# Diffusion transformer blocks on one core: keys and self queries as products of 512 columns, and another order of the steps

## The reference

```
shift_sa, scale_sa, gate_sa, shift_ff, scale_ff, gate_ff = split(silu(cond) @ ada_w + ada_b, 6)
x = x + gate_sa * (attn(LN(x) * (1 + scale_sa) + shift_sa; qkv_w) @ sa_proj_w + b)
x = x + attn(q from LN(x), k and v from ctx, masked) @ ca_proj_w + b
x = x + gate_ff * (gelu((LN(x) * (1 + scale_ff) + shift_ff) @ fc1_w + b) @ fc2_w + b)
```

## Time and profile before

| | us |
|---|---|
| median of 3 runs | 1639.54 (1636.42 to 1641.39) |
| the profiled execution | 1635.45 |
| its span, first to last instruction | 1633.6 |
| mean granted clock of TensorE, as a share | 0.985 |
| busy: PE / DVE / ACT / POOL | 1470.9 / 1116.5 / 951.1 / 719.8 |
| PE share of the chain that ended last | 62% |
| "issue" share of it | 9% |

### The profile page before, as it was taken

One profiled execution on the slowest core, in us unless ns is written; L12 is line 12 of the kernel. 1 busy time (PEld: TensorE's weight loads), 2 busy tenths in 40 slices (PEclk: granted clock), 3 DMA queues, 4 the chain that ended last, 5 costly groups with the idle time before them and its releaser, 6 DMA issues.

```text
span 1633.6 us, 44574 instructions
## 1 busy us (share of the span) xinstructions
PE 1470.9 (90%) x17632; PEld 1282.0 (78%) x17632; DVE 1116.5 (68%) x2407; ACT 951.1 (58%) x1754; POOL 719.8 (44%) x982
## 2 busy tenths in 40 slices
PE   5979999999999999999888889989898898989987
PEld 4868878788887878888787777868778787887867
DVE  5557766666776666667766777677777767677654
ACT  3456565666656566665656646566565566656543
...
DMA packets 34251, 49.38 MB, mean 30 GB/s; under 512 B 3488, under 2 KB 24928, under 8 KB 34048
## 3 DMA queue, kind: packets, MB, share of 16 engines
...
...
## 4 chain that ended last, share of the span: by engine, by line
PE 62%; DVE 18%; ACT 9%; issue 9%; POOL 1%; SPq 0%; DMA 0%; DVEq 0%; ACTq 0%; POOLq 0%
PE score_t L676 8%; PE score L655 6%; PE p_unit L549 6%; PE p_unit L745 5%; PE p_mix L718 5%; PE p_unit L551 4%; PE p_unit L550 4%; DVE neg_max L1119 4%; PE p_out L549 3%; PE p_out L551 3%; PE p_out L550 3%; DVE hid_hi L1164 2%; PE p_mix L580 2%; DVE hid_lo L1166 2%; PE p_turn L735 2%
## 5 line engine op out<-in xcount | busy, mean ns | idle before, releaser
L1119 DVE TENSOR_REDUCE neg_max<-score 128x8 f32<-128x1024 f32 x224 | 273.8, 1222 | 115.2 <-PE score L655 109.7
L655 PE MATMUL score<-k_t,q_t 32*128 32x256 f32 x1792 | 254.5, 401 | 41.3 <-DVE q_less L1129 14.2
L676 PE MATMUL score_t<-q_less,k_t 32*128 32x128 f32 x3584 | 264.9, 287 | 11.5 <-ACT probs_t L977 6.1
L676 PEld LDWEIGHTS score_t<-q_less,k_t 32*128 32x128 f32 x3584 | 222.1, 189 | 23.3 <-issue 21.1
L979 ACT ACTIVATE probs_t<-score_t 128x1024 f32<-128x1024 f32 x168 | 172.0, 1024 | 94.4 <-PE score_t L676 81.7
L655 PEld LDWEIGHTS score<-k_t,q_t 32*128 32x128 f32 x1792 | 163.7, 188 | 77.7 <-issue 36.6
L1323 POOL TENSOR_TENSOR xt_lo<-xt,xt_hi 128x256 fp32r<-128x256 f32 x128 | 94.7, 740 | 261.8 <-ACT xt_hi L903 260.3
L898 ACT ACTIVATE xt<-p_mix,mod_now 128x128 f32<-128x128 f32 x384 | 154.3, 454 | 91.9 <-PE p_mix L580 60.6
L745 PE MATMUL p_unit<-w_out,heads_t 128*128 128x256 f32 x512 | 145.2, 407 | 21.0 <-ACT q_t L942 8.2
L549 PE MATMUL p_out<-w_hi,hid_lo 128*128 128x256 f32 x512 | 151.5, 296 | 0.8 <-issue 0.8
L1166 DVE TENSOR_TENSOR hid_lo<-hid,hid_hi 128x256 fp32r<-128x256 f32 x256 | 145.1, 567 | 8.8
...
## 6 DMA issues: line engine op xcount, KB each, us to landing
...
```

What stands on the lines that cost most here:

```text
L655: mm = pe.matmul(score_banks(b, h)[:, r % 2, t * 2 * N:(t + 1) * 2 * N].rearrange("p (e n) -> p e n", e=2), q_t[s][rows(r), t, tokens], k_ ...
L676: mm = pe.matmul(turned_banks(b, h)[:, r % 2, x * N:(x + 1) * N], k_t[s][rows(r), t, e, tokens], q_less[rows(r), j % 2, t, e, :], start=Tr ...
L1119: dve.tensor_reduce(by_half[:, 2 * h:2 * h + 2, 0:CT, :], score_banks(b, h)[:].rearrange("p r (t e n) -> p r t e n", t=CT, e=2), AX.X, ALU ...
```

## The change

Keys of both attentions and self queries become "by tile": such a unit holds one block of 128 features for all 4 batches, 2 x 3 = 6 products of 512 columns, where it held two blocks for 2 batches. They need the normed rows of all 4 batches, and the first round of an attention needs both key units (and both self query units). ACT and DVE move such a unit in one operation of 512 columns in place of two of 256; POOL's rotation takes the same number of elements in another shape.

The order changes on every engine. ACT moves a unit one step later, but first in that step (`ACT_UNIT` 1); then keys, context, gelus, exps, modulation, heads, mix, and the table loads last. On PE turn_heads moves ahead of norm, turn_max behind the MLP, the first norm ahead of turn_back. DVE scales keys first in a step, and heads ahead of z; POOL rotates ahead of the inverse roots and casts the context last. Units move (`UNIT_STEPS`), the MLP's 32 items stand in steps 36 to 43 and not 36 to 45, so a group ends two steps earlier; the keys' lag is 3; the context is split in step 20 and not 22; the copies of the modulation rows move; z of the first norm stands in the step of its transpose. In group 0 the statistics begin at step -16, the gates at -6, and the low weights of chunk 0 come at step -8, behind the first modulation.

```diff
-ACT_MIX, ACT_UNIT, ACT_MOD, ACT_HI = 0, 0, 0, 0
-DVE_KEYS, DVE_LOW, DVE_SCALE, DVE_SWAP, DVE_OUT = 1, 4, 1, 1, 0
+ACT_MIX, ACT_UNIT, ACT_MOD, ACT_HI = 0, 1, 0, 0
+DVE_KEYS, DVE_LOW, DVE_SCALE, DVE_SWAP, DVE_OUT = 1, 3, 1, 1, 0
...
-KEYS_LAG = 4
-FIRST_STATS, FIRST_Z, FIRST_LNT = -12, -11, -10
-AT_CTX = -4
+KEYS_LAG = 3
+FIRST_STATS, FIRST_Z, FIRST_LNT = -12, -10, -10
+EARLY_STATS = -16
+AT_CTX = -6
...
-MOD_AT = (-15, -1, 24)
+MOD_AT = (-20, -9, 26)
...
+def by_tile(unit):
+    return unit[0] == "k" or unit[:2] == ("q", SELF)
...
-UNIT_STEPS = ((-6, -5, -1, 2, 3, 4, 6, 7, 11, 14, 16, 18),
-              (-6, -5, -1, 2, 3, 4, 6, 7, 11, 14, 16, 17))
+UNIT_STEPS = ((-6, -5, -3, -1, 2, 4, 6, 7, 11, 15, 16, 18),
+              (-6, -5, -4, -2, -1, 4, 6, 7, 11, 14, 16, 17))
...
-MLP_COUNTS = ((2, 0, 3, 8, 2, 6, 7, 2, 1, 1), (2, 1, 2, 7, 6, 5, 5, 2, 1, 1))
+MLP_COUNTS = ((2, 1, 9, 3, 1, 4, 9, 3), (2, 3, 13, 0, 4, 1, 5, 4))
...
-GATES_AT, MOD_FF_AT, BIAS_AT, MOD_LN_AT, MOD_ROWS_AT = -1, 2, 6, 10, 11
+GATES_AT, MOD_FF_AT, BIAS_AT, MOD_LN_AT, MOD_ROWS_AT = -6, 4, 6, 10, 13
...
-FIRST_LO_DVE_AT = {-10: 0, -4: 1, 6: 3}
+FIRST_LO_DVE_AT = {-8: 0, -4: 1, 6: 3}
...
-PE_ORDER = ("round", "max", "proj", "norm", "mlp", "back", "turn", "first", "mix", "unit")
+PE_ORDER = ("round", "proj", "turn", "norm", "mlp", "max", "first", "back", "mix", "unit")
...
                 else:
-                    pe.wait_ge(xt_hi_made[s], group * 4 + 2 * half + 2)
-                    pe.wait_ge(xt_lo_made[s], group * 4 + 2 * half + 2)
+                    batches = GB if by_tile(UNITS[n]) else 2 * half + 2
+                    pe.wait_ge(xt_hi_made[s], group * 4 + batches)
+                    pe.wait_ge(xt_lo_made[s], group * 4 + batches)
...
-                for part in range(2):
+                for part in range(1 if by_tile(UNITS[n]) else 2):
                     for c in range(CT):
+                        if by_tile(UNITS[n]):
+                            mm = product(p_unit[:], w(col, c, stride, at + half * P, P), (hi[:, c, :], lo[:, c, :]),
+                                         c == 0, c == CT - 1)
+                            continue
...
             def scores(group, s, b, h):
 
                 if b % 2 == 0 and h == 0:
-                    half = b // 2
-                    pe.wait_ge(keys_low, group * 4 + 2 * s + half + 1)
-                    pe.wait_ge(keys_high, group * 4 + 2 * s + half + 1)
-                    pe.wait_ge(queries_made, group * 4 + 2 * s + half + 1)
+                    if b == 0:
+                        pe.wait_ge(keys_low, group * 4 + 2 * s + 2)
+                        pe.wait_ge(keys_high, group * 4 + 2 * s + 2)
+                    pe.wait_ge(queries_made, group * 4 + 2 * s + (2 if s == SELF else b // 2 + 1))
                     if b == 0 and s == CROSS and group:
...
                     for group, step in live(t):
-                        for s, b in batch_at(step, AT_TURN_MAX):
-                            turn_max(group, 4 * s + b)
-                    for group, step in live(t):
                         for s, b in batch_at(step, AT_PROJ):
                             project(group, s, b)
+                    for group, step in live(t):
+                        for s, b in batch_at(step, AT_TURN_Q):
+                            turn_heads(group, 4 * s + b)
...
                     for group, step in live(t):
+                        for s, b in batch_at(step, AT_TURN_MAX):
+                            turn_max(group, 4 * s + b)
+                    for group, step in live(t):
+                        for b in first_at(step, FIRST_LNT):
+                            turn_z(group, 0, b)
+                    for group, step in live(t):
                         for s, b in batch_at(step, AT_TURN_BACK):
                             turn_back(group, 4 * s + b)
-                    for group, step in live(t):
-                        for s, b in batch_at(step, AT_TURN_Q):
-                            turn_heads(group, 4 * s + b)
-                    for group, step in live(t):
-                        for b in first_at(step, FIRST_LNT):
-                            turn_z(group, 0, b)
                     for group, step in live(t):
...
-                    last = (group - 1) * 8 + 4 * s + 2 * half + 2
...
+                elif unit[:2] == ("q", SELF):
+                    act.activation(q_t[s][:, half, :], p_unit[:], ACT.Identity, scale=SCALE,
+                                   bias=bias_cols[:, 4 + half:5 + half]).then_inc(queries_made, 1)
...
                 else:
-                    for t in range(CT):
-                        op = act.activation(k_t[s][:, t, 0, cols], p_unit[:, t * HALF:(t + 1) * HALF], ACT.Identity,
-                                            scale=head_mask[:, 0:1], bias=key_bias[:, 0, 2 * s + t:2 * s + t + 1])
-                    op.then_inc(keys_low, 1)
+                    act.activation(k_t[s][:, half, 0, :], p_unit[:], ACT.Identity, scale=head_mask[:, 0:1],
+                                   bias=key_bias[:, 0, 2 * s + half:2 * s + half + 1]).then_inc(keys_low, 1)
...
                     for group, step in live(t):
+                        if step - ACT_UNIT in UNIT_AT[layer_of(group)]:
+                            move_unit(group, UNITS.index(UNIT_AT[layer_of(group)][step - ACT_UNIT]))
+                    for group, step in live(t):
+                        if layer_of(group) == 1 and step in KEYS_AT:
+                            low_keys(group, KEYS_AT[step])
+                    for group, step in live(t):
                         if step == AT_CTX:
                             split_ctx(group)
                         if (group, step) in SPLIT_AT:
                             new_weights((group, step))
                     for group, step in live(t):
-                        if layer_of(group) == 1 and step in KEYS_AT:
-                            low_keys(group, KEYS_AT[step])
+                        for n in GELU_AT[layer_of(group)].get(step, ()):
+                            gelu(group, n)
                     for group, step in live(t):
                         for s, b, h in turned_score_at(step):
                             exps(group, s, b, h)
                     for group, step in live(t):
-                        for n in GELU_AT[layer_of(group)].get(step, ()):
-                            gelu(group, n)
+                        for k, b in normed_at(step, AT_LNT + ACT_MOD, FIRST_LNT + ACT_MOD):
+                            modulate(group, k, b)
+                    for group, step in live(t):
+                        for s, b in batch_at(step, AT_TURN_BACK + ACT_HI):
+                            move_heads(group, 4 * s + b)
+                    for group, step in live(t):
+                        for s, b in batch_at(step, AT_MIX + ACT_MIX):
+                            move_mix(group, 4 * s + b)
...
                             act.activation(primed[:], cond[:, 0, 0:1], ACT.Exp)
-                    for group, step in live(t):
-                        for s, b in batch_at(step, AT_TURN_BACK + ACT_HI):
-                            move_heads(group, 4 * s + b)
-                    for group, step in live(t):
-                        for s, b in batch_at(step, AT_MIX + ACT_MIX):
-                            move_mix(group, 4 * s + b)
-                    for group, step in live(t):
-                        for k, b in normed_at(step, AT_LNT + ACT_MOD, FIRST_LNT + ACT_MOD):
-                            modulate(group, k, b)
-                    for group, step in live(t):
-                        if step - ACT_UNIT in UNIT_AT[layer_of(group)]:
...
                 dve.wait_ge(keys_low, group * 4 + 2 * s + half + 1)
-                for t in range(CT):
-                    op = dve.tensor_scalar(k_t[s][:, t, 1, half * HALF:(half + 1) * HALF],
-                                           p_unit[:, t * HALF:(t + 1) * HALF], head_mask[:, 1:2],
-                                           key_bias[:, 1, 2 * s + t:2 * s + t + 1], ALU.mult, ALU.add)
-                op.then_inc(keys_high, 1)
+                dve.tensor_scalar(k_t[s][:, half, 1, :], p_unit[:], head_mask[:, 1:2],
+                                  key_bias[:, 1, 2 * s + half:2 * s + half + 1], ALU.mult, ALU.add).then_inc(keys_high, 1)
 
...
                 for t in STEPS:
-                    if t in FIRST_LO_DVE_AT:
...
+                    for group, step in live(t):
+                        if layer_of(group) == 1 and step in KEYS_AT:
+                            high_keys(group, KEYS_AT[step])
+                    for group, step in live(t):
+                        for s, b in batch_at(step, AT_TURN_Q + DVE_SCALE):
+                            scale_heads(group, 4 * s + b)
                     for group, step in live(t):
                         for k, b in normed_at(step, AT_Z, FIRST_Z):
                             normalise(group, k, b)
                     for group, step in live(t):
```

(12 more changed lines are left out.)

42 lines of the change are left out of this document (19 added, 23 removed).

## The result

The kernel after takes 1628.12 us (median of 6 runs, 1624.81 to 1633.55), the kernel before 1638.45 in the same runs (1636.42 to 1641.39). The ratio is 0.9942 [0.9927, 0.9957]: 10 us faster, where 44 were forecast (1594 against 1638 to 1640). The profiled execution took 1624.81 us, span 1623.0, mean granted clock 0.962 (before: 0.985).

What follows compares the result with a forecast made beforehand. PE, busy 90% of the span, was taken as the bound. 8 x 2.8 (layer 0) + 8 x 3.1 (layer 1) = 47.2 us less, 2 more: profiled 1635.45 to 1590.2; median 4.1 above, 1594. Range 1566 to 1636.

Steps and rivals of the forecast that it cites:

- The products' 0.42: Six of twelve units, as 6 products of 512 columns for 12 of 256, save PE 0.42 us a group.
- 0.6 + 0.33 + 0.42 - 0.4: Layer 0: shorter evictions at steps 20-21 (0.6) and 6-7 (0.33), wide products (0.42), less the key unit's four-batch wait (0.4).
- The statement on steps 19 and 20: Layer 0: PE's waits of 0.30 and 0.25 us for the maximum and exps would go; 0.55 us gained.
- the moved MLP fillers of steps 18 and 19: Layer 1: MLP products taken from these steps return only part of their 1.4 us; 1.0 us a period lost.
- The gains of the list: Layer 1: six PE gaps (1.35, 0.85, 0.76, 0.73, 0.64, 1.16 us) would go, 5.49 us a period.
- The splits of step 12: Layer 1: DVE's hidden-unit splits, held by POOL's rotation of cross keys, come late; 0.9 us booked, bounds 0 and 3.
- The 0.25 and 0.3 booked around step 21: Layer 1 losses: the round behind the first key unit waits for DVE (0.25 us); step 21's shuffle delays a maximum (0.3).
- Start: Earlier modulation and statistics gain up to 2.6 us, but first scores need four units, all batches; loss of 2 taken.
- Rival 1: POOL's work from step 18 to round 1 binds layer 1 and eats its gain: 1619 us; chance 0.13.
- Rival 2: Layer 1: POOL's rotations each wait for the previous one's key scaling, slipping over 6 us: 1646 us; chance 0.12.
- Rival 3: Waits only move: filler from steps 18 and 19 costs 1.4 us in both layers, key unit waits 1.5: 1637; chance 0.06.
- Rival 4: Wide products run at the far faster pitch, 0.55 us a unit more, times 96: 1541 us; chance 0.04.

Runs made afterwards that it cites:

- last experiment: The second kernel with layer 0's second key unit in step 22 and not 23: 1607.93 us, ratio 0.9828 to the kernel before.
- fourth: The kernel after with every unit by halves again (256 columns), the new order kept: 1623.4 us, ratio 0.9914 to the kernel before.
- fifth experiment: The second kernel with layer 0's last two MLP items also moved to steps 18 and 19: 1609.34 us, ratio 0.9831 to the kernel before.
- first kernel: The kernel after with useless PE transposes added in layer 1, 12 in step 18 and 6 in step 19: 1618.71 us, ratio 0.9889.
- the second: The kernel after with two of layer 1's four step-17 MLP items put back to steps 18 and 19: 1604.96 us, ratio 0.9802.
- the sixth: The kernel before with only the change's new MLP counts, so the MLP ends at step 17: 1647.13 us, ratio 1.0066.
- third kernel: The kernel after with POOL's two sums of the MLP output in layer 1 one step later: 1619.52 us, ratio 0.9903 to the kernel before.
- eighth experiment: The kernel of the fifth experiment with DVE's layer 1 shuffle behind the maximum's subtraction: 1636.14 us, ratio 1.0006 to the kernel before.
- ninth kernel: The second kernel with the gate products of group 0 at step -1 again, not -6: 1603.38 us, ratio 0.98 to the kernel before.

## Why the prediction was wrong

The direction and the range held (1628 lies in 1566 to 1636), the size did not: 10 us for 44. By its steps:

- **Layer 0: right in its sum, in part by luck.** 2.8 us a period were forecast, 2.4 came (95.34 to 92.95). The products' 0.42 are 0. Other terms missed and cancelled. Shown: the wait at step 24 is filled by the unit of step 23 (0.7 us, last experiment), the eviction and the width, less the wait for four batches, give 0.3 (fourth), where 0.6 + 0.33 + 0.42 - 0.4 was booked. ACT and DVE take 0.776 and 0.803 us for a key unit, 0.61 less than the two pairs of the earlier trace rows, where 0.7 was taken (groups by line and shape, kernel after):

```profile
L963 ACT ACTIVATE k_t<-p_unit,key_bias,head_mask 128x512 f32<-128x512 f32 x32 | 24.8, 776 | 23.9 <-PE p_unit L560 23.9
```

```profile
L1102 DVE TENSOR_SCALAR k_t<-p_unit,head_mask,key_bias 128x512 f32<-128x512 f32 x32 | 25.7, 803 | 26.9 <-ACT k_t L963 26.9
```

The statement on steps 19 and 20 was wrong: instead of going, 0.30 and 0.25 became 1.05 and 0.26. It cost little, as the fifth experiment shows, for a round there follows the maximum in any case. The other way went the norm of step 13, whose 0.29 us for z closed without being booked, the projection, 0.56 for 0.42, and the 0.25 for steps 4 and 6, of which no row is left.
- **Layer 0, what is missing.** 6 x -2.8 = -16.8 was forecast, -9.2 came: 2.1 are the products in five periods, 3.2 the sixth, at the seam, which got 0.4 longer where 2.8 less was forecast, and 2.2 the two periods at a clock of 0.98.
- **Layer 1: the step that failed.** It is the sentence "the moved MLP fillers of steps 18 and 19 return only part of their 1.4 us (1.0 lost)". The gains of the list did come: the six gaps closed, and PE's idle time fell by 2.37 us a period where the terms for waits gave 5.49 - 2.8 = 2.69. But PE's busy time, forecast 0.42 lower, rose by 2.25. The working priced the filler as PE time that overlaps a wait. It had no term for what an idle PE does to its own clock, 1.25 us a period, and none for POOL's queue, 1.34. Together the moved items cost 2.6 us a period, not 1.0; with them back the period is 95.6, 2.7 under that of before. The clock's share is shown by the first kernel, whose periods differ from the kernel after behind the key unit alone. That moving the items costs time, in the old order too, is shown by the second (23 us less) and the sixth (11 us more).
- **POOL's queue.** The output sums follow the MLP, and now stood ahead of a rotation and of the low part that ACT waits for. That queue was not walked through at step 19. That it holds the key unit's input is shown by the third kernel, where the input ends 1.26 us earlier.
- **Layer 1, smaller terms.** The unit of step 20 waits 0.38 us for the booked 0.35, but only because PE comes late to it; at the full clock it waits 1.44 (first kernel). The splits of step 12 take 1.37 to 1.52 us each under POOL's rotation, in place of 0.28 and 0.43, as forecast, and PE waits 0.63 us for one where 0.9 was booked. The round of step 3 now waits 0.78 us for the queries less their maximum; before, it had no such row, and units stood in steps 2 and 3. The prediction booked the like of it in layer 0 only. The 0.25 and 0.3 booked around step 21 have no rows.
- **Start: -3 to +5 with a loss of 2 taken, +1.0 measured** at the first Exp load. This can't be called right or wrong. Six runs have the code of the kernel after up to there (it, the first, second, third, fifth and eighth), and their first Exp load stands at 184.86 to 192.58 us, the kernel before's at 186.91. Their first round is 5 to 8 us later than before; much of it is made up.
- **The end: 0 forecast; the last stretch is 1.8 us longer**, with as many products (592) and a clock of 0.83 for 0.88. The second and the ninth kernel, with the same code there, take 68.00 us at 0.90 and 65.84 at 0.95. So this row too is the clock's, and differs from run to run.
- **Rival 1 (POOL binds layer 1)** is not what happened: POOL's last addition ends 0.9 us ahead of round 1, by its walk 0.8. But its mechanism is real and near, as the eighth experiment shows: there its price is 3.3 us a period, and it begins at step 20, ahead of where the rival looked. **Rival 2**: the steps between rotations didn't add up to a slip of 6 us. **Rival 3** came nearest in kind: the filler costs more than its length; it had 0.06. Its 1637 does not follow from its words: 1.4 us of filler in both layers for 0 and 1.0, and 1.5 at the key unit for 0.4 and 0.35, add 32 us to 1594, which is 1626. That this lies near 1628 is luck, for layer 0's filler costs nothing and layer 1's more. **Rival 4** is refuted.
- **What would show it.** "It is wrong if PE's busy time falls by over 1 us a period": PE's busy time rose by 2.25 in layer 1, a sign that the prediction had not thought of.

What stays open: how the remaining gain divides between PE's order, the step tables, and the orders of DVE and POOL. Only ACT's order was tried by itself. A kernel with the old orders of DVE and POOL was not run, nor one with the useless work and POOL's sums later, which would part the two causes without moving an MLP item.
